# Second-layer attention product with tiles of the probabilities as weights and the solution moving

## Chip, cores and metric

The kernel runs on one core of a Trainium2 chip. The metric is the device time of one execution in microseconds (us); a kernel's time is the median of its runs. The core has five engines with queues of their own that work in order and wait for one another by semaphores: TensorE (PE in the profile, its weight loads PEld), VectorE (DVE), ScalarE (ACT), GpSimd (POOL) and SyncE (SP, which issues DMAs).

## What is computed

Two transformer layers on x of shape (4, 256, 256). Each layer has an attention and a feed-forward part, each fed by a gated recurrence over time (`cond`). In the second layer the attention doesn't multiply the probabilities with the values but with the solution u of a triangular system for each of the 16 heads (head width 16), and the feed-forward part routes each token to two of eight experts. The part that the change touches, in the reference:

```python
p = e / where(denom == 0, 1, denom)              # keys against earlier keys, row sums 1
A = p * beta + eye(T)                            # lower triangular, 256 x 256 for each head
u = solve_triangular(A, v, lower=True)
attn = softmax(where(causal, q k^T * scale, -inf))
o = einsum('bhij,bhjd->bihd', attn, u).reshape(B, T, 256)
return o @ Wo
```

## The kernel before

The four batches are worked one after the other. A list of steps, ORDER, gives the order on every engine; each engine walks through it and does its part of each step. DVE uses a variant (DVE_ORDER, made by `lag`) in which steps that don't belong to the chain of a solve are held back behind the chain's steps while a solve is under way.

The solve of a batch goes by blocks of 32 rows: `inverse` (DVE transposes the inverted diagonal blocks that POOL has worked out, L1845), `solve` (PE multiplies a block, DVE copies the result to `ublk`, L1867, SP moves it with four DMAs, L866, to `uaug`/`uflat`, where tokens lie on partitions) and `update` (PE, L1138; DVE, L1853 and L1856) in turn, eight blocks in two halves. Other work of the batches around it (scores and probabilities, projections, `oT` and `wo` of the batch before) is spread between the chain's steps by `spread`.

Behind each chain stands `pv`, the product of probabilities and solution, on PE in two steps of eight heads (L1054 to L1070). The probabilities `prob` lie with keys on partitions, in full floats and not yet divided by their sums. For each head the weights are 32 columns of `uflat` (16 of the solution, one of ones that yields the sum, 15 that belong to the next head), and the moving operand is `prob[:, h, 0:256]` for the first 128 keys and the last 128 queries for the other keys. The outputs of four heads lie in four groups of 32 partitions of a PSUM bank, so a head's values come out on partitions and the queries along the row. Both steps wait for all 32 DMAs of the solution (`u_moved`).

Then ACT copies each half to SBUF (L1421, `oraw`), PE transposes it back in eight 128x128 pieces (`otr`, L1081), and DVE takes the reciprocal of the sums from PSUM (L1734) and multiplies (L1735) into `otok`, which has queries on partitions. `oT` (L1091) transposes `otok` for the output projection `wo`. For batches 0 to 2 the `otr` steps lie among the steps of the next batch's chain; for the last one they follow at once. The next batch's `inverse` and `solve` follow `pv` in ORDER; for batches 0 and 1 some of the `kprobs` steps stand around it, and ahead of the last `pv` stand three `route` steps (tokens as 128x128 float weights, 8 columns of the gate moving) and `count`.

PSUM banks are handed out by rings: a step takes the next slot of its ring and waits until the engine named in RINGS has given it back. `mm` (L904) issues every product, so in the profile most products have one line.

Of the kernel before, what the change touches and what calls it, by code (L numbers as in the profile page):

```python
# [33 lines left out]
ALU = mybir.AluOpType  # L34
# [57 lines left out]
    ("kscores", None): ("mid", ("act",)), ("kdiag", None): ("mid", ("act",)), ("kprobs", None): ("mid", ("act",)),  # L92
    ("pv", 0): ("big", ("act",)), ("pv", 1): ("mid", ("act",)),
    ("otr", 0): ("big", ("dve",)), ("otr", 1): ("mid", ("dve",)),
    ("oT", 0): ("big", ("act",)), ("oT", 1): ("mid", ("act",)),
# [159 lines left out]
def make_order():  # L255
# [12 lines left out]

    def otr(b):
        return [[("otr", 1, b, 0)], [("otr", 1, b, 1)]]  # L270

    def keys_then_queries(b):
# [19 lines left out]
    def inverted(b):  # L292
# [4 lines left out]
             + queries(1),  # L297
             k3 + otr(0) + d3 + p1[:4] + [[("oT", 1, 0)]] + p1[4:8] + out(0)[1:] + p1[8:] + [[("qload", 3)]] + queries(2),
             otr(1) + p2[:4] + [[("oT", 1, 1)]] + p2[4:8] + out(1)[1:] + p2[8:]
             + queries(3),  # L300
             otr(2) + p3[:4] + [[("oT", 1, 2)]] + p3[4:8] + out(2)[1:] + p3[8:]]
    for b in range(B):

# [11 lines left out]
    last = sum(out(B - 1), [])  # L315
    o += [("wfirst", 0, 0), ("otr", 1, B - 1, 0), ("otr", 1, B - 1, 1), ("wsplit", 0, 0), last[0], ("wfirst", 0, 1)] + last[1:]
    o += [("wfirst", 1, 0), ("wsplit", 0, 1), ("route", B - 1)] + [("ytok", i) for i in range(B)] + [("xtok", i) for i in range(B)]
# [113 lines left out]
def program(nc, d):  # L431

    with ExitStack() as ctx:
# [104 lines left out]

        def oraw(layer, b):


            return v3(oraw0 if layer == 0 else invT[b % 2], 4)


        top_all = top[0]
# [29 lines left out]
        tern_flat = take(CT * HID, at=r1 + 4 * (H * T // 2))  # L575
        oraw0 = take(QT * H * 32, at=r1 + 5 * (H * T // 2))
        hid = v3(tern_flat, MT)
# [146 lines left out]
        pad_ready = sem("zero_columns_ready")  # L724
        u_moved = sem("solution_moved")

# [42 lines left out]
        def _(sp):  # L769
# [38 lines left out]
            for step in ORDER:  # L808
# [86 lines left out]
        def _(pe):  # L895
# [14 lines left out]
            for step in ORDER:  # L910
# [143 lines left out]
                elif kind == "pv":  # L1054
# [3 lines left out]
                    if layer == 0:  # L1058
                        wait_done(pe, ("proj", 0, b), "dve")
                        val = vflat[b % NV]  # L1060
                    else:
                        pe.wait_ge(u_moved, 16 * HQ * NS * (b + 1))
                        val = uflat
                    slot = acquire(step)
                    for h in range(step[3] * H // 2, (step[3] + 1) * H // 2) if layer else range(H):
                        out = (bank_of(slot) if layer else wide(slot)[:, h // 8, :]).rearrange("p (g t) -> p g t", g=2)[
                            (h % 4) * 32:(h % 4) * 32 + 32, h // 4 % 2, :]
                        mm(out, val[:, h * VW:h * VW + 32], prob[:, h, 0:T], True, False)
                        at = (H + h) * VW
                        last = mm(out[:, P:T], val[:, at:at + 32], prob[:, h, T:T + P], False, True)  # L1070
                    wrote(step, last)
                elif kind == "otr":

                    layer, b = step[1:3]
                    wait_done(pe, ("pv", layer, b, 1) if layer else ("pv", 0, b), "act")
                    slot = acquire(step)
                    raw = oraw(layer, b)
                    for t in step[3:] if layer else range(QT):
                        out = bank_of(slot) if layer else wide(slot)[:, t, :]
                        for g in range(4):  # L1080
                            last = nc.tensor.transpose(out[:, g * P:(g + 1) * P], raw[:, g, t * P:(t + 1) * P],  # L1081
                                                       ident)
                    wrote(step, last)
                elif kind == "oT":
                    _, layer, b = step
                    wait_done(pe, ("otr", 1, b, 1) if layer else ("otr", 0, b), "dve")
                    slot = acquire(step)
# [175 lines left out]
        def _(act):  # L1263
# [23 lines left out]
            for step in ORDER:  # L1287
# [109 lines left out]
                elif kind == "kscores":  # L1397
# [11 lines left out]
                    give_back(step, ins)  # L1409
                elif kind == "pv":  # L1410
                    layer, b = step[1:3]
                    slot = filled(step)
                    if layer == 0:
                        if b:
                            wait_pe(act, ("otr", 0, b - 1))
                    else:
                        wait_pe(act, ("solve", b, NS - 1, 1))
                        act.wait_ge(invT_ready, b + 1)
                    if layer:
                        half = slice(2 * step[3], 2 * step[3] + 2)  # L1420
                        give_back(step, A(oraw(layer, b)[:, half, :], bank_of(slot).rearrange("p (g t) -> p g t", g=2), ACT.Copy))  # L1421
                    else:
                        give_back(step, A(oraw(layer, b), wide(slot).rearrange("p a (g t) -> p (a g) t", g=2), ACT.Copy))
                elif kind == "oT":
# [94 lines left out]
        def _(dve):  # L1519
# [50 lines left out]
            for step in DVE_ORDER:  # L1570
# [139 lines left out]
                elif kind == "minus":  # L1710
# [11 lines left out]
                    V.tensor_tensor(lo, v3(mneg, QT), hi, ALU.subtract).then_inc(mparts_ready["max"], 1)  # L1722
                elif kind == "otr":
                    layer, b = step[1:3]
                    slot = filled(step)
                    n = layer * B + b
                    ts = slice(step[3], step[3] + 1) if layer else slice(0, QT)
                    nt = ts.stop - ts.start
                    o_ = (v3(bank_of(slot), 1) if layer else wide(slot)).rearrange("p t (h e) -> p t h e", h=H)
                    if n:  # L1730
# [4 lines left out]
                    give_back(step, V.tensor_tensor(otok[:, ts].rearrange("p t (h e) -> p t h e", h=H), o_[:, :, :, 0:HD],  # L1735
                                                    r_.unsqueeze(3).to_broadcast([P, nt, H, HD]), ALU.mult))
                elif kind == "wo":
# [101 lines left out]
                elif kind == "inverse":  # L1839
# [340 lines left out]
```

## Time and profile before

| | us |
|---|---|
| median of 3 runs | 781.09 (777.92 to 781.1) |
| the profiled execution | 783.57 |
| its span, first to last instruction | 781.8 |
| PE busy with products | 512.3 |
| PE busy with weight loads | 416.5 |
| DVE busy | 566.9 |
| ACT busy | 329.5 |
| POOL busy | 214.1 |

The second layer's solves and attention lie between about 425 and 640 us of the span. Times in rows count from the start of the span. Each float product on PE shows as two rows, a pass each, with a weight load of its own. "128*32" is the part of the array that a product uses (rows times columns), "128x256" the moving operand. PEclk is the granted clock of TensorE as a share of 2.4 GHz; it has two levels, 1.0 and 0.5. "idle before" in brackets is how long the engine stood still and what ended that.

### The profile page before, as it was taken

How to read it: one execution, taken by the hardware profiler on the slowest of the kernel's cores; microseconds unless marked ns; L12 is line 12 of the kernel's file. 1: busy time of each engine (PE TensorE's matmuls, PEld its weight loads, DVE VectorE, ACT ScalarE, POOL GpSimd, SP SyncE). 2: the span in 40 equal slices, each digit the busy share in tenths (PEclk: the TensorE clock that was granted, in tenths of full speed). 3: DMA queues.
4: the chain of work that ended last, by engine and by line, in shares of the span. 5: the costliest groups of instructions: out<-in, count | busy, mean ns of one | idle time of the engine just before them, and what ended most of it. 6: DMA issues, size and time to landing. Idle time of an engine off the chain costs nothing.

```text
span 781.8 us, 17527 instructions
## 1 busy us (share of the span) xinstructions
PE 512.3 (66%) x7117; PEld 416.5 (53%) x7117; DVE 566.9 (73%) x1184; ACT 329.5 (42%) x779; POOL 214.1 (27%) x313
## 2 busy tenths in 40 slices
PE   0451754895595853444647577758887873799995
PEld 0341643784485742332435355536654653799995
DVE  6899599797859994678676877666475446768861
ACT  4335243453355622006365611433411343368771
POOL 3000000000000000000685881880683001325443
PEclk9965656896798977665667676659898856699999
DMA  8055005032000020175007133002202238256622
GB/s 310 22 118 122 0 18 105 1 85 38 1 2 1 1 55 0 49 156 122 4 3 158 13 75 61 7 5 49 64 10 63 31 143 283 88 153 204 191 29 27
DMA packets 48209, 56.02 MB, mean 72 GB/s; under 512 B 25136, under 2 KB 42048, under 8 KB 43648
## 3 DMA queue, kind: packets, MB, share of 16 engines
q1 hardware_dynamic: 44784, 49.90, 24.7%
q0 software_dynamic: 3344, 4.99, 3.4%
q8 instruction: 56, 0.92, 0.5%
q14 instruction: 25, 0.20, 0.1%
HBM read 43.15 MB, written 10.49 MB: 69 GB/s over the span
## 4 chain that ended last, share of the span: by engine, by line
PE 37%; DVE 27%; issue 8%; ACT 4%; DMA 1%; POOL 1%; SPq 0%; POOLq 0%; DVEq 0%; ACTq 0%
PE psum L904 32%; DVE arena L1705 3%; PE psum L1138 3%; DVE arena L1687 2%; DVE arena L1856 2%; ACT psum L1408 1%; DVE arena L1692 1%; DVE arena L1695 1%; DVE arena L1693 1%; DVE arena L1853 1%; DVE arena L1590 1%; DVE arena L1618 1%; DVE arena L1634 1%; DVE psum L1654 1%; DVE arena L1655 1%
## 5 line engine op out<-in xcount | busy, mean ns | idle before, releaser
L904 PE MATMUL psum<-arena 32*32 32x16 f32 (+20 forms) x5281 | 354.6, 278 | 192.1 <-DVE arena L1634 76.6
L904 PEld LDWEIGHTS psum<-arena 98*32 98x32 bf16 (+8 forms) x5281 | 273.6, 128 | 269.7 <-DVE arena L1634 79.3
L2086 POOL TENSOR_TENSOR arena<-arena 128x31 f32<-128x31 f32 (+15 forms) x124 | 69.0, 556 | 9.7
L1705 DVE TENSOR_REDUCE arena<-psum 128x4 f32<-128x1024 f32 (+2 forms) x80 | 59.7, 789 | 11.6 <-PE psum L904 11.1
L1373 ACT ACTIVATE arena<-psum 128x512 f32<-128x512 f32 (+1 forms) x80 | 50.5, 687 | 40.0 <-PE psum L904 40.0
L2084 POOL TENSOR_TENSOR arena<-arena 128x31 f32<-128x31 f32 (+15 forms) x124 | 64.4, 520 | 9.7
L1408 ACT ACTIVATE psum<-psum,arena 128x256 f32<-128x256 f32 (+7 forms) x128 | 45.3, 367 | 27.8 <-DVE arena L1695 27.5
L1604 DVE TENSOR_TENSOR_SCAN arena<-arena 128x255 f32<-128x255 f32 x64 | 42.5, 727 | 11.4 <-ACT arena L1318 11.3
L2065 POOL DMA_DIRECT2D arena<-wq x1 | 0.9, 862 | 171.9 <-PE psum L904 171.9
L1318 ACT ACTIVATE arena<-arena 128x255 f32<-128x255 f32 x64 | 27.2, 498 | 46.4 <-DVE arena L1590 46.4
L2110 POOL DMA_INDIRECT out<-arena x16 | 31.2, 1948 | 48.9 <-DVE arena L2010 46.8
L2100 POOL DMA_INDIRECT arena<-dispatched,arena x16 | 19.6, 1227 | 84.7 <-DVE arena L1977 81.0
L1992 DVE TENSOR_TENSOR fc_second_parts<-arena,fc_first_parts 128x2048 fp32r<-128x2048 f32 x16 | 36.6, 2290 | 7.8 <-ACT fc_first_parts L1515 7.7
L904 PE MATMUL psum<-input_first_parts,fc_first_parts 128*128 128x256 f32 x128 | 39.0, 305 | 1.3 <-DVE input_second_parts L1986 1.3
L1487 ACT ACTIVATE psum<-psum,arena 128x256 f32<-128x256 f32 x64 | 24.6, 448 | 35.7 <-PE psum L904 35.7
L1138 PE MATMUL psum<-arena 32*32 32x224 f32 (+6 forms) x896 | 36.2, 307 | 5.0 <-DVE arena L1867 3.0
L1590 DVE TENSOR_TENSOR_SCAN arena<-arena 128x256 f32<-128x256 f32 x64 | 39.0, 672 | 0.5
L904 PE MATMUL psum<-fc_first_parts,hidden_first_parts 128*128 128x256 f32 x128 | 36.8, 288 | 2.5 <-DVE hidden_second_parts L2003 2.5
L904 PE MATMUL psum<-input_second_parts,fc_first_parts 128*128 128x256 f32 x128 | 38.2, 299 | 0.0
L904 PE MATMUL psum<-input_first_parts,fc_second_parts 128*128 128x256 f32 x128 | 38.2, 298 | 0.0
L904 PE MATMUL psum<-fc_first_parts,hidden_second_parts 128*128 128x256 f32 x128 | 36.2, 283 | 0.0
L904 PE MATMUL psum<-fc_second_parts,hidden_first_parts 128*128 128x256 f32 x128 | 36.2, 283 | 0.0
(185 smaller groups left out, 890.4 us busy)
## 6 DMA issues: line engine op xcount, KB each, us to landing
arena<-fc SPq DMA_DIRECT2D x16, 1024.0 KB, 5.0
arena<-parts SPq DMA_DIRECT2D x40, 256.0 KB, 4.6
parts<-arena SPq DMA_DIRECT2D x16, 384.0 KB, 3.6
arena<-parts SPq DMA_DIRECT2D x40, 128.0 KB, 5.5
arena<-arena SPq DMA_DIRECT2D x128, 8.0 KB
arena<-xT SPq DMA_DIRECT2D x1, 1024.0 KB, 10.4
arena<-w1T SPq DMA_DIRECT2D x1, 1024.0 KB, 10.8
arena<-w2T SPq DMA_DIRECT2D x1, 1024.0 KB, 13.0
```

What stands on the lines that cost most here:

```text
L904: return nc.tensor.matmul(out, lhsT, rhs, start=start, stop=stop)
L1138: last = nc.tensor.matmul(acc(half)[rows, qq, (s + 1) * BLK:T], ublk[rows, s, q, :], later[b % 2][s][rows, q, :], start=s == 0 and qq == 0 ...
L1318: A(scan[s + 1][:, ct, 0:T - 1], scan[s][:, ct, 0:T - 1], ACT.Copy, scale=back[:, i:i + 1]).then_inc(scaled, 1)
L1373: ins = A(prob[:, first:end, 0:T] if early else prob[:, first:end, T:T + P], src, ACT.Exp, scale=scale)
L1408: ins = A(s_, s_, ACT.Exp, bias=nbias[:, n:n + 1], accum_out=ncc[b][:, n:n + 1])
L1590: ins = V.tensor_tensor_scan(scan[s][:, ct, :], dd, src[:, ct, bt(b)], 0.0, ALU.mult, ALU.add)
L1604: st(V.tensor_tensor_scan(scan[s][:, ct, T - 2::-1], dd, scan[s + 1][:, ct, T - 2::-1], scan[s][:, ct, T - 1:T], ALU.mult, ALU.add))
L1705: ins = V.tensor_reduce(mneg[:, at + first:at + end], src, axis=AX.X, op=ALU.max, negate=True)
L1992: V.tensor_tensor(second[:], fcw[e % NW][i], first[:].bitcast(F32), ALU.subtract).then_inc(w_second[i], 1)
L2084: link(G_.tensor_tensor(tmp, A3[:, k + 1:BLK, k:k + 1].to_broadcast([P, rows, w]), X3[:, k:k + 1, 0:w].to_broadcast([P, rows, w]), ALU.mult))
L2086: ins = G_.tensor_tensor(X3[:, k + 1:BLK, 0:w], X3[:, k + 1:BLK, 0:w], tmp, ALU.add)
L2110: G_.indirect_dma_start(out=d["out"], out_offset=bass.IndirectOffsetOnAxis(ap=ids[:, 2 * e + s:2 * e + s + 1], axis=0), in_=eo[e % 2][:, s ...
```

## The change

In the second layer `pv` is done with the operands in each other's place: the weights are a 128x128 tile of `prob` (128 keys by 128 queries of one head), the moving operand is the 17 columns of a head in `uflat` (16 of the solution and the one of ones). The two steps of `pv` are now the two halves of the queries, each for all 16 heads, with queries on partitions: the first has one tile of keys, the second two, which add up in PSUM. DVE reads the result where `pv` has left it and takes the reciprocal and the product as before. The `otr` steps of the second layer go, and with them ACT's copies; `pv` is given back by DVE and so stands in DVE's order, right behind the chain and ahead of the next `inverse`. The semaphore `u_moved` becomes one for each tile of 128 keys. `inverse` of a later batch waits for the last `solve` instead of `otr`, and at the end ACT's first conversion of expert weights waits for the last `pv`. The first layer stays as it is. The diff, cut to its core:

```diff
-    ("pv", 0): ("big", ("act",)), ("pv", 1): ("mid", ("act",)),
-    ("otr", 0): ("big", ("dve",)), ("otr", 1): ("mid", ("dve",)),
+    ("pv", 0): ("big", ("act",)), ("pv", 1): ("mid", ("dve",)),
+    ("otr", 0): ("big", ("dve",)),
...
-             k3 + otr(0) + d3 + p1[:4] + [[("oT", 1, 0)]] + p1[4:8] + out(0)[1:] + p1[8:] + [[("qload", 3)]] + queries(2),
-             otr(1) + p2[:4] + [[("oT", 1, 1)]] + p2[4:8] + out(1)[1:] + p2[8:]
+             k3 + d3 + p1[:4] + [[("oT", 1, 0)]] + p1[4:8] + out(0)[1:] + p1[8:] + [[("qload", 3)]] + queries(2),
+             p2[:4] + [[("oT", 1, 1)]] + p2[4:8] + out(1)[1:] + p2[8:]
              + queries(3),
-             otr(2) + p3[:4] + [[("oT", 1, 2)]] + p3[4:8] + out(2)[1:] + p3[8:]]
+             p3[:4] + [[("oT", 1, 2)]] + p3[4:8] + out(2)[1:] + p3[8:]]
...
-    o += [("wfirst", 0, 0), ("otr", 1, B - 1, 0), ("otr", 1, B - 1, 1), ("wsplit", 0, 0), last[0], ("wfirst", 0, 1)] + last[1:]
+    o += [("wfirst", 0, 0), last[0], ("wsplit", 0, 0), ("wfirst", 0, 1)] + last[1:]
...
-        u_moved = sem("solution_moved")
+        u_moved = [sem(f"solution_tile{t}_moved") for t in range(QT)]
...
-                                     ).then_inc(u_moved, 16)
+                                     ).then_inc(u_moved[t], 16)
...
                     else:
-                        pe.wait_ge(u_moved, 16 * HQ * NS * (b + 1))
-                        val = uflat
-                    slot = acquire(step)
-                    for h in range(step[3] * H // 2, (step[3] + 1) * H // 2) if layer else range(H):
-                        out = (bank_of(slot) if layer else wide(slot)[:, h // 8, :]).rearrange("p (g t) -> p g t", g=2)[
-                            (h % 4) * 32:(h % 4) * 32 + 32, h // 4 % 2, :]
-                        mm(out, val[:, h * VW:h * VW + 32], prob[:, h, 0:T], True, False)
-                        at = (H + h) * VW
-                        last = mm(out[:, P:T], val[:, at:at + 32], prob[:, h, T:T + P], False, True)
+                        t = step[3]
+                        slot = acquire(step)
+                        for kt in range(t + 1):
+                            pe.wait_ge(u_moved[kt], 16 * HQ * NB * (b + 1))
+                            for h in range(H):
+                                at = (kt * H + h) * VW
+                                queries = slice(T, T + P) if kt else slice(t * P, (t + 1) * P)
+                                last = mm(bank_of(slot)[:, h * VW:(h + 1) * VW], prob[:, h, queries], uflat[:, at:at + VW],
+                                          kt == 0 and h == 0, kt == t and h == H - 1)
...
-                        wait_pe(act, ("solve", b, NS - 1, 1))
-                        act.wait_ge(invT_ready, b + 1)
-                    if layer:
-                        half = slice(2 * step[3], 2 * step[3] + 2)
-                        give_back(step, A(oraw(layer, b)[:, half, :], bank_of(slot).rearrange("p (g t) -> p g t", g=2), ACT.Copy))
...
                 elif kind == "wfirst" or kind == "wsplit" and step[1] >= 2:
                     _, e, i = step
+                    if e == 0:
+                        wait_pe(act, ("pv", 1, B - 1, 1))
...
-                elif kind == "otr":
+                elif kind == "otr" or kind == "pv" and step[1]:
...
-                    o_ = (v3(bank_of(slot), 1) if layer else wide(slot)).rearrange("p t (h e) -> p t h e", h=H)
+                    if layer:
+                        o_ = v3(bank_of(slot)[:, 0:H * VW], 1).rearrange("p t (h e) -> p t h e", h=H)
...
                     if b >= 2:
-                        wait_pe(dve, ("otr", 1, b - 2, 1))
+                        wait_pe(dve, ("solve", b - 2, NS - 1, 1))
...
                     if b and s == 0:
-                        dve.wait_ge(u_moved, 16 * HQ * NS * b)
+                        for t in range(QT):
+                            dve.wait_ge(u_moved[t], 16 * HQ * NB * b)
```

## Rows read from the trace of the kernel before

**Rows 1.** The page: its first line, and the chain that ended last, by engine.

```profile
span 781.8 us, 17527 instructions
...
PE 512.3 (66%) x7117; PEld 416.5 (53%) x7117; DVE 566.9 (73%) x1184; ACT 329.5 (42%) x779; POOL 214.1 (27%) x313
...
PE 37%; DVE 27%; issue 8%; ACT 4%; DMA 1%; POOL 1%; SPq 0%; POOLq 0%; DVEq 0%; ACTq 0%
```

**Rows 2.** Timeline after batch 0: start, us, engine, line, op, tiles, xcount [idle before].

```profile
488.57 6.60 PE L904 MATMUL psum<-arena 128*32 128x256 f32 x152 [1.01 <-issue]
...
493.89 0.60 ACT L1421 ACTIVATE arena<-psum 128x512 f32<-128x512 f32 x1 [1.83 <-PE psum L904]
...
494.55 0.30 DVE L1867 COPY arena<-psum 128x32 f32<-128x32 f32 x2 [7.83 <-PE psum L904]
```

**Rows 3.** Timeline, handover after batch 1.

```profile
549.45 1.97 DVE L1845 STREAM_TRANSPOSE arena<-arena 128x1024 f32<-128x1024 f32 x1
...
551.57 1.91 POOL L2077 TENSOR_TENSOR arena<-arena 128x1024 f32<-128x1024 f32 x1 [22.08 <-DVE arena L1845]
...
552.48 0.24 PEld L904 LDWEIGHTS psum<-arena 128*32 128x32 f32 x4 [0.18 <-issue]
...
557.42 0.29 DVE L1867 COPY arena<-psum 128x32 f32<-128x32 f32 x2 [6.00 <-PE psum L904]
```

**Rows 4.** Timeline, handover after batch 2.

```profile
589.71 0.31 PE L1033 MATMUL psum<-arena 128*64 128x128 bf16 x1 [2.50 <-DVE arena L1722]
...
593.35 1.97 DVE L1845 STREAM_TRANSPOSE arena<-arena 128x1024 f32<-128x1024 f32 x1 [3.69 <-POOL arena L2086]
...
596.88 0.30 DVE L1867 COPY arena<-psum 128x32 f32<-128x32 f32 x2 [1.56 <-PE psum L904]
```

**Rows 5.** Timeline, last batch: routing, product, normalising, transposition of the result.

```profile
619.08 11.48 PE L904 MATMUL psum<-arena 32*32 32x16 f32 x113 [0.26 <-DVE arena L1856]
...
632.08 0.26 DVE L1734 RECIPROCAL arena<-psum 128x16 f32<-128x16 f32 x1 [6.05 <-PE psum L1081]
...
632.37 0.42 DVE L1735 TENSOR_TENSOR arena<-psum,arena 128x256 f32<-128x256 f32 x1
...
633.47 0.72 PEld L1091 LDWEIGHTS psum<-arena 128*128 128x128 f32 x4 [1.29 <-DVE arena L1735]
```

**Rows 6.** Groups by form, 625.5 to 630.6: shapes, xcount, busy us, mean ns.

```profile
L904 PEld LDWEIGHTS psum<-arena 128*32 128x32 f32 x64 | 3.0, 159 | 1.8 <-issue 1.5
```

**Rows 7.** Stretches: us, busy PE, PEld, DVE, ACT, POOL, PEclk, DMA, GB/s.

```profile
488.60:493.80 5.20, 5.20 (x81) 3.68 (x85) 0.00 (x0) 0.72 (x2) 4.44 (x10) 0.53 0.00 0
...
501.00:524.00 23.00, 10.79 (x301) 7.22 (x302) 16.23 (x50) 11.90 (x60) 20.41 (x34) 0.50 0.05 5
...
597.00:619.00 22.00, 19.05 (x488) 12.73 (x488) 12.86 (x63) 7.19 (x13) 0.00 (x0) 1.00 0.12 13
...
620.40:625.20 4.80, 4.80 (x25) 4.79 (x24) 0.70 (x4) 0.67 (x2) 0.00 (x0) 0.50 0.39 72
...
625.60:630.60 5.00, 4.96 (x65) 3.03 (x64) 0.35 (x2) 0.88 (x2) 0.00 (x0) 0.56 1.02 431
```

**Rows 8.** Groups by form, 620.3 to 625.2, the routing products.

```profile
L904 PEld LDWEIGHTS psum<-arena 128*128 128x128 f32 x24 | 5.4, 333 | 0.1
...
L904 PE MATMUL psum<-arena 128*128 128x8 f32 x24 | 5.1, 355 | 0.0
```

**Rows 9.** Timeline, a transposition of the second layer at full clock.

```profile
597.26 0.42 PEld L1081 LDWEIGHTS psum<-arena 128*128 128x128 f32 x4 [0.48 <-ACT arena L1421]
```

**Rows 10.** Timeline of PE alone: products of the chains of batches 1 and 3.

```profile
524.05 2.36 PE L1138 MATMUL psum<-arena 32*32 32x160 f32 x32 [1.78 <-issue]
...
597.85 1.72 PE L1138 MATMUL psum<-arena 32*32 32x224 f32 x32
...
615.90 0.45 PE L1138 MATMUL psum<-arena 32*32 32x32 f32 x32
```

**Rows 11.** Timeline, products of ranks with bf16 weights.

```profile
648.42 1.21 PEld L904 LDWEIGHTS psum<-arena 128*128 128x128 bf16 x40
```

More of the change, by code:

```diff
@@ L267, in pv @@
         return [("pv", 1, b, 0), ("pv", 1, b, 1)]
-    def otr(b):
-        return [[("otr", 1, b, 0)], [("otr", 1, b, 1)]]
     def keys_then_queries(b):
@@ L537, in program @@
         top[0] = max(top[0], e_end)
-        def oraw(layer, b):
-            return v3(oraw0 if layer == 0 else invT[b % 2], 4)
         top_all = top[0]
@@ L575, in program @@
         tern_flat = take(CT * HID, at=r1 + 4 * (H * T // 2))
-        oraw0 = take(QT * H * 32, at=r1 + 5 * (H * T // 2))
+        oraw0 = v3(take(QT * H * 32, at=r1 + 5 * (H * T // 2)), 4)
         hid = v3(tern_flat, MT)
@@ new lines, in _ @@
+                        for h in range(H):
+                            out = wide(slot)[:, h // 8, :].rearrange("p (g t) -> p g t", g=2)[(h % 4) * 32:(h % 4) * 32 + 32, h // 4 % 2, :]
+                            mm(out, val[:, h * VW:h * VW + 32], prob[:, h, 0:T], True, False)
+                            at = (H + h) * VW
+                            last = mm(out[:, P:T], val[:, at:at + 32], prob[:, h, T:T + P], False, True)
+                    else:
+                        t = step[3]
+                        slot = acquire(step)
+                        for kt in range(t + 1):
+                            pe.wait_ge(u_moved[kt], 16 * HQ * NB * (b + 1))
+                            for h in range(H):
+                                at = (kt * H + h) * VW
+                                queries = slice(T, T + P) if kt else slice(t * P, (t + 1) * P)
+                                last = mm(bank_of(slot)[:, h * VW:(h + 1) * VW], prob[:, h, queries], uflat[:, at:at + VW],
+                                          kt == 0 and h == 0, kt == t and h == H - 1)
@@ L1071, in _ @@
                     wrote(step, last)
                 elif kind == "otr":
-                    layer, b = step[1:3]
-                    wait_done(pe, ("pv", layer, b, 1) if layer else ("pv", 0, b), "act")
+                    _, layer, b = step
+                    wait_done(pe, ("pv", layer, b), "act")
                     slot = acquire(step)
-                    raw = oraw(layer, b)
-                    for t in step[3:] if layer else range(QT):
-                        out = bank_of(slot) if layer else wide(slot)[:, t, :]
+                    raw = oraw0
@@ L1080, in _ @@
+                    for t in range(QT):
                         for g in range(4):
-                            last = nc.tensor.transpose(out[:, g * P:(g + 1) * P], raw[:, g, t * P:(t + 1) * P],
+                            last = nc.tensor.transpose(wide(slot)[:, t, g * P:(g + 1) * P], raw[:, g, t * P:(t + 1) * P],
                                                        ident)
@@ L1085, in _ @@
                     _, layer, b = step
-                    wait_done(pe, ("otr", 1, b, 1) if layer else ("otr", 0, b), "dve")
+                    wait_done(pe, ("pv", 1, b, 1) if layer else ("otr", 0, b), "dve")
                     slot = acquire(step)
@@ L1409, in _ @@
                     give_back(step, ins)
-                elif kind == "pv":
-                    layer, b = step[1:3]
+                elif kind == "pv" and step[1] == 0:
+                    b = step[2]
                     slot = filled(step)
[L1413 to L1416, printed above, removed]
-                        wait_pe(act, ("solve", b, NS - 1, 1))
-                        act.wait_ge(invT_ready, b + 1)
-                    if layer:
-                        half = slice(2 * step[3], 2 * step[3] + 2)
-                        give_back(step, A(oraw(layer, b)[:, half, :], bank_of(slot).rearrange("p (g t) -> p g t", g=2), ACT.Copy))
-                    else:
-                        give_back(step, A(oraw(layer, b), wide(slot).rearrange("p a (g t) -> p (a g) t", g=2), ACT.Copy))
+                    if b:
+                        wait_pe(act, ("otr", 0, b - 1))
+                    give_back(step, A(oraw0, wide(slot).rearrange("p a (g t) -> p (a g) t", g=2), ACT.Copy))
                 elif kind == "oT":
@@ L1727, in _ @@
                     ts = slice(step[3], step[3] + 1) if layer else slice(0, QT)
-                    nt = ts.stop - ts.start
-                    o_ = (v3(bank_of(slot), 1) if layer else wide(slot)).rearrange("p t (h e) -> p t h e", h=H)
+                    if layer:
+                        o_ = v3(bank_of(slot)[:, 0:H * VW], 1).rearrange("p t (h e) -> p t h e", h=H)
+                    else:
+                        o_ = wide(slot).rearrange("p t (h e) -> p t h e", h=H)
                     if n:
@@ L1735, in _ @@
                     give_back(step, V.tensor_tensor(otok[:, ts].rearrange("p t (h e) -> p t h e", h=H), o_[:, :, :, 0:HD],
-                                                    r_.unsqueeze(3).to_broadcast([P, nt, H, HD]), ALU.mult))
+                                                    r_.unsqueeze(3).to_broadcast([P, ts.stop - ts.start, H, HD]), ALU.mult))
                 elif kind == "wo":
@@ L1865, in _ @@
                     if b and s == 0:
-                        dve.wait_ge(u_moved, 16 * HQ * NS * b)
+                        for t in range(QT):
+                            dve.wait_ge(u_moved[t], 16 * HQ * NB * b)
                     give_back(step, V.tensor_copy(ublk[:, s, half * QP:(half + 1) * QP, 0:HD],
```

## The prediction

> **What bounds the kernel now.** I read the page first: the span, the busy shares and the chain that ended last. No engine is full (TensorE, PE in the rows, is busy 66% of the 781.8 us), but the chain lies on PE for 37% and on VectorE (DVE) for 27% [rows 1]: work is handed to and fro, and time counts where the chain passes. So I went by the timeline to the four places where the change acts, the second layer's attention product `pv` of each of the four batches. In the first three, one solve chain has just ended and the next one starts with `inverse` (a transposition on DVE) and `solve`, whose first result is copied by L1867; on PE's queue, which runs in the order of ORDER, the next `solve` stands behind `pv`. The reader is to see in [rows 2 to 4] that PE has nothing beside `pv` there: batch 0's product starts at 488.57, after 1.01 us of waiting for the last rows of the solution, its second eviction starts at 493.89, and the next chain's first copy comes at 494.55. In the last batch [rows 5] PE runs without a gap from 619.08 to 630.56 (three `route` steps, then `pv`), then an eviction, eight transpositions, and normalising on DVE before `oT` starts at 633.47. So `pv` is on the path in all four places, and what it costs on PE is paid in full.
>
> Then I asked the list of groups by form what one `pv` is now, and the view by stretches which clock it gets. It is 64 loads of 128x32 weights [rows 6], because each of its 32 float products is done in two passes; four of them stand side by side in the array. The last batch's fills a stretch of 5.0 us, the first one's 5.2 us, both at a granted clock just over 0.5, that is 1.2 GHz for most of it [rows 7]. Its end is later followed by full clock: 597 to 619 has 1.00 [rows 7].
>
> **The change part by part.** *The product.* Per batch the new `pv` does 16 heads for the first half of the queries and 2 x 16 for the second: 48 products, each with a 128x128 tile of probabilities as weights and 17 columns moving. In two passes that is 96 loads of 128x128 float weights. The trace of before has the same load with almost as few moving columns: `route`, 128x128 float weights and 8 columns. There, 24 passes kept PE busy 5.1 us [rows 8], 0.2125 us each, with no idle time, at clock 0.50 [rows 7]. The moving columns don't show in that pace: one load lasts 333 ns on average [rows 8], longer than the distance to the next, so loads set it. I take the same price for 17 columns: 96 x 0.2125 = 20.4 us for a batch, where 5.0 to 5.2 us stood. A lower bound for a pass is the full-clock row: four 128x128 float loads of a transposition took 0.42 us [rows 9] in a stretch at clock 1.00 [rows 7], 0.105 each, 10.1 us for a batch. An upper bound is a little over the 0.2125. I take the end at half rate, because `route` is the same form, and because it shows what such a stream does to the clock: it ran 4.8 us without a gap and stayed at 0.50 [rows 7], and the old `pv` that followed was still mostly there. The stretches ahead of `pv` are sparse, as they are now, and nothing in the change makes them denser, so it starts at the low level too.
>
> The Trainium skill (TensorE: Matmul & The Clock Gate, section on what is actually happening) says that sustained matmul activity releases the throttle. By that rule the new `pv`, four times as long as the old one and without a gap, would run at 2.4 GHz for most of its length; the `route` stretch at 0.50 [rows 7] speaks against it. The same page (section LDWEIGHTS) prices a load by its columns over 1.2 GHz, an estimate of 107 ns for 128 of them; the `route` row [rows 8] has twice that. By either the sum would be that of the first rival below.
>
> *The wait for the solution.* The semaphore is split by tile, and only the last third of `pv` needs the second tile. The 1.01 us of batch 0 [rows 2] goes, and in batch 2 `pv` can start right after 590.02, where PE's last step ahead of it ends [rows 4]. Nothing is queued behind this wait that could gain more.
>
> *The handover to the next chain.* ACT's two copies and the eight transpositions go; DVE now reads PSUM, a reciprocal and a multiplication for each half, 0.26 and 0.42 us [rows 5]. The first half's lie under PE, the second's 0.7 us follow PE's end. This is a new place on DVE's queue: `inverse` of the next batch stands behind `pv`, so DVE waits for PE some 20 us with the transposition of 1.97 us [rows 3] queued behind it, and PE's first `solve` waits for that. Before, it was done while PE multiplied or waited. From the end of `pv` to the first copy of the next chain I count 0.7 + 1.97 + 0.6 (a `solve` and its handover, an estimate from the 0.66 us between the last eviction's start and the copy, 493.89 to 494.55 [rows 2]) = 3.3 us.
>
> Now the four places, new against old:
> - batch 0: 487.56 + 20.4 + 3.3 = 511.3 against 494.55 [rows 2], +16.7
> - batch 1: 552.48 + 20.4 + 3.3 = 576.2 against 557.42 [rows 3], +18.8
> - batch 2: 590.02 + 20.4 + 3.3 = 613.7 against 596.88 [rows 4], +16.8
> - batch 3: the old product's end, 630.56, less its 5.0 [rows 5, 7], is 625.6; 625.6 + 20.4 + 0.7 = 646.7 against 633.47 for `oT` [rows 5], +13.2
>
> Together +65.5 us. GpSimd's inversion of a batch starts when the one before is handed over (551.57 [rows 3]) and ends at 593.35 [rows 4], some 42 us, which made DVE wait 3.69 us in batch 2. It starts late now too, but the chain plus the longer `pv` that it has to be ready for is longer by 20 us, so it stays covered; were it not, it would cost what is left of 3.69 us.
>
> *What the chains gain.* In the chains of batches 1 to 3 the eight transpositions (twice 0.42 us at full clock [rows 9]) and DVE's two pairs (1.36 us [rows 5]) no longer stand among the steps: at most 2.2 us a chain, nothing where they filled a wait. I take 1.3 for each, -4 us, with 0 and -6.6 as ends.
>
> *What the clock does afterwards.* The old `pv` ended with the clock on its way up. After a stream like `route` the next chain starts at the low level. A step of the chain's products took 2.36 us with 160 columns in chain 1, at the low level, and 1.72 with 224 in chain 3, at the high one [rows 7, 10]: 14.8 ns a column against 7.7. Chain 3 has seven such rows, from 1.72 down to 0.45 us [rows 10], 7.5 us together, of 19.05 us that PE is busy there [rows 7]. A whole chain at half rate would lose 7.5 us on these and, as I estimate, 5 of the 11.5 on the rest, the remainder lying in waits for DVE. Chain 1 is mostly low already (501 to 524 at 0.50 [rows 7]), so two chains bear it: 0 to 25 us. I take +7, under a third, since the `proj`, `probs` and `wo` steps that lie in these chains are those in which the clock stands high now.
>
> The rest has one answer: SP's semaphores count differently but the same DMAs go out at the same steps; ACT's first conversion of expert weights waits for the end of `pv`, where it stood behind the copies of the same product; the PSUM ring has two uses fewer per batch. I cost these at nothing, because `oT`, `wo` and the gate follow in the same order and hide the conversions as now.
>
> Sum: 65.5 - 4 + 7 = +68.5 us. The profiled execution took 783.57 us around its span of 781.8; the median of the three runs is 781.09, 2.5 below it. On the profiled execution the sum gives 852, on the median 849.6; I forecast 850.
>
> **The rivals.**
> 1. *The stream itself lifts the clock.* Then a pass costs 0.105 us [rows 9], a `pv` 10.1 us instead of 20.4, and nothing is lost afterwards: 65.5 - 4 x 10.3 - 4 = +20.3, 801 us; lifted for part of each batch, 812 to 840. For it: four places of 20 us of dense PE, more than any stretch there now. Against it: `route` [rows 7]. It decides from the batch in which the clock rises within the stream. This is also the time by the two rules of the skill.
> 2. *Faster: loads at the price of bf16.* The table of ranks does 40 passes with 128x128 bf16 weights in 1.21 us [rows 11], 0.03 each. At that price a new `pv` is 2.9 us: 65.5 - 4 x 17.5 - 4 = -8.5, 773 us. It decides below about 0.05 us for a pass, where 65.5 - 4 is paid back over 384 passes. Against it: the operands stay float, and the float row with 8 columns is at 0.2125. Only if the second pass reused a loaded tile, or loads lay side by side, could it come near.
> 3. *The low clock spreads.* The chains of batches 2 and 3 stay at half rate to their ends, and the dense stretches after them too: +25 instead of +7 and more, 868 us and above.
>
> That the change doesn't do what it says is hardly a case: the rows of the copies and of `otr` can't stay, since the steps are gone from the order.
>
> **How the numbers follow.** Forecast (half rate, 850, its own range 840 to 871): 0.70. Rival 1: 0.20, of which 0.08 for full rate throughout and 0.12 for part. Rival 2: 0.04, nearly all of it faster. Rival 3: 0.06. The range from 812 to 870 leaves out the full-rate case, rival 2 and most of rival 3, 0.18 or so. A measurement of this kernel can tell about 0.5% (4 us) from no change; faster 0.03, same 0.01, slower 0.96.
>
> **What would show it.** In the profile of after: a group of 128x128 float loads with 17 columns, 384 passes in all, four stretches of about 20 us of PE with a granted clock of 0.50 (rival 1: 1.00 and 10 us); DVE idle for most of each, ended by PE, and `inverse` right behind; no gap on PE ahead of `pv` in batch 0; the four shifts near 17, 19, 17 and 13 us; low clock at the start of the chains of batches 2 and 3. I am wrong if the stream's pace with 17 columns isn't that with 8, or if PE's queue lets other work in between.

## The result and the profile after

The changed kernel takes 848.63 us (843.05 to 852.44), the kernel before 779.77 beside it: a ratio of 1.0875, 95% interval 1.0836 to 1.0914. The profiled execution took 849.38 us around a span of 847.6, with a mean granted clock of 0.751 (before: 0.774).

The page of after: span, busy times, and the group in which DVE's waiting now lies.

```profile
span 847.6 us, 17700 instructions
...
PE 571.7 (67%) x7213; PEld 480.5 (57%) x7213; DVE 568.2 (67%) x1184; ACT 324.5 (38%) x771; POOL 214.8 (25%) x313
...
L1727 DVE RECIPROCAL arena<-psum 128x16 f32<-128x16 f32 (+1 forms) x12 | 3.4, 286 | 84.5 <-PE psum L895 84.5
```

Against [rows 1] PE is busy 59.4 us longer and its weight loads 64.0 us, while DVE is nearly as before (1.3 us more) and ACT 5.0 us shorter (the copies that went). DVE's 84.5 us of waiting ahead of the reciprocals of the second layer (two for each `pv`; the other four are the first layer's) all end with a product: this is the four new `pv`, seen from their reader.

The stretches of after: the four `pv`, then the start and the rest of the chains of batches 2 and 3. Columns as in [rows 7].

```profile
488.40:509.00 20.60, 20.60 (x104) 20.56 (x104) 0.68 (x2) 1.20 (x6) 0.00 (x0) 0.50 0.00 1
567.70:588.30 20.60, 20.60 (x100) 20.56 (x104) 0.68 (x2) 1.35 (x6) 0.00 (x0) 0.50 0.16 53
624.90:645.60 20.70, 20.69 (x97) 20.55 (x96) 0.68 (x2) 0.27 (x1) 6.65 (x17) 0.50 0.16 53
677.70:698.30 20.60, 20.60 (x98) 20.49 (x97) 1.03 (x4) 0.28 (x1) 0.00 (x0) 0.50 0.36 139
591.50:596.80 5.30, 5.30 (x47) 2.50 (x43) 2.42 (x8) 1.16 (x2) 4.76 (x7) 0.50 0.07 6
596.80:622.40 25.60, 20.78 (x506) 14.15 (x505) 19.04 (x62) 6.46 (x13) 22.58 (x38) 1.00 0.10 10
648.80:651.60 2.80, 2.64 (x36) 1.35 (x32) 0.93 (x5) 0.00 (x0) 0.00 (x0) 0.52 0.08 12
651.60:672.00 20.40, 17.58 (x477) 11.63 (x470) 11.21 (x54) 7.57 (x13) 0.00 (x0) 1.00 0.12 12
```

Each `pv` fills PE for 20.6 us at the lower level, where [rows 7] has 5.0 and 5.2 (and the old `pv` of batch 1 took 3.8). The last four lines show what is left of that level behind it: the chains of batches 2 and 3 run their first 5.3 and 2.8 us at 0.50 and the rest at 1.00.

The groups by form of after: a `pv` of batch 0, and all 384 passes of the second layer.

```profile
L895 PE MATMUL psum<-arena 128*128 128x17 f32 x96 | 20.7, 375 | 0.0
L895 PEld LDWEIGHTS psum<-arena 128*128 128x128 f32 x96 | 20.6, 333 | 0.1
...
L895 PE MATMUL psum<-arena 128*128 128x17 f32 x384 | 82.6, 375 | 0.0
```

It is 82.6 / 384 = 0.215 us a pass. A load again lasts longer (333 ns) than the distance to the next, as in [rows 8].

The timeline of after: the handovers behind batches 0 and 2 and the step to `oT` in the last batch.

```profile
486.01 23.89 PE L895 MATMUL psum<-arena 98*32 98x224 bf16 x208
...
495.41 0.26 DVE L1727 RECIPROCAL arena<-psum 128x16 f32<-128x16 f32 x1 [9.71 <-PE psum L895]
...
509.07 0.26 DVE L1727 RECIPROCAL arena<-psum 128x16 f32<-128x16 f32 x1 [12.94 <-PE psum L895]
509.36 0.42 DVE L1728 TENSOR_TENSOR arena<-psum,arena 128x256 f32<-128x256 f32 x1
...
509.70 1.90 DVE L1838 STREAM_TRANSPOSE arena<-arena 128x1024 f32<-128x1024 f32 x1
511.65 1.39 PEld L895 LDWEIGHTS psum<-arena 32*32 32x32 f32 x56 [1.97 <-DVE arena L1838]
...
512.19 0.35 DVE L1861 COPY arena<-psum 128x32 f32<-128x32 f32 x2 [0.59 <-DVE arena L1838]
...
645.63 0.26 DVE L1727 RECIPROCAL arena<-psum 128x16 f32<-128x16 f32 x1 [12.94 <-PE psum L895]
...
646.26 1.89 DVE L1838 STREAM_TRANSPOSE arena<-arena 128x1024 f32<-128x1024 f32 x1
...
648.75 0.35 DVE L1861 COPY arena<-psum 128x32 f32<-128x32 f32 x2 [0.59 <-DVE arena L1838]
...
673.79 24.51 PE L895 MATMUL psum<-arena 128*128 128x8 f32 x115
...
698.34 0.26 DVE L1727 RECIPROCAL arena<-psum 128x16 f32<-128x16 f32 x1 [12.88 <-PE psum L895]
...
699.11 0.72 PEld L1087 LDWEIGHTS psum<-arena 128*128 128x128 f32 x4 [0.92 <-DVE arena L1728]
```

The first line is `kprobs` of batch 1 and `pv` of batch 0 without a gap, so the 1.01 us of [rows 2] is gone. At 509.07 PE is done, DVE normalises, and only then its transposition comes (L1838, `inverse`), with PE waiting 1.97 us for it. The first copy of the next chain stands at 512.19, where [rows 2] has 494.55. Behind batch 2 it is the same picture. In the last batch `oT` starts at 699.11.

The whole, cut at the first and last copy of each chain (L1861 in after, L1867 in before):

| | before | after | difference |
|---|---|---|---|
| start to first copy of chain 0 | 427.30 | 428.18 | +0.9 |
| chains 0, 1, 2, 3 | 55.48, 52.34, 30.11, 22.58 | 55.49, 50.59, 30.90, 23.26 | 0.0, -1.75, +0.8, +0.7 |
| handovers behind batches 0, 1, 2 | 11.77, 10.52, 9.36 | 28.52, 28.68, 26.38 | +16.75, +18.2, +17.0 |
| last copy of chain 3 to the end | 162.29 | 175.56 | +13.3 |

The four places of the change make up 65.2 of the 65.8 us between the spans.

### The profile page after: what moved, and what is told of

It reads as the page before. It is cut to its first block and busy times, and to the rows that moved or that the text cites. A ratio compares the mean times of both kernels' runs of the same rounds, so it can differ in the third digit from the quotient of the medians.

```text
span 847.6 us, 17700 instructions
## 1 busy us (share of the span) xinstructions
PE 571.7 (67%) x7213; PEld 480.5 (57%) x7213; DVE 568.2 (67%) x1184; ACT 324.5 (38%) x771; POOL 214.8 (25%) x313
## 5 line engine op out<-in xcount | busy, mean ns | idle before, releaser
L895 PE MATMUL psum<-arena 32*32 32x16 f32 (+21 forms) x5409 | 416.8, 276 | 199.6 <-DVE arena L1624 76.5
L895 PEld LDWEIGHTS psum<-arena 128*128 128x128 f32 (+8 forms) x5409 | 341.8, 142 | 271.0 <-DVE arena L1624 79.2
L1695 DVE TENSOR_REDUCE arena<-psum 128x4 f32<-128x1024 f32 (+2 forms) x80 | 59.8, 788 | 10.8 <-PE psum L895 10.4
L1727 DVE RECIPROCAL arena<-psum 128x16 f32<-128x16 f32 (+1 forms) x12 | 3.4, 286 | 84.5 <-PE psum L895 84.5
L1505 ACT ACTIVATE fc_first_parts<-arena 128x2048 fp32r<-128x2048 f32 x16 | 30.6, 1910 | 32.6 <-PE psum L895 32.6
L1134 PE MATMUL psum<-arena 32*32 32x224 f32 (+6 forms) x896 | 39.4, 323 | 4.8 <-DVE arena L1861 4.7
L2071 POOL TENSOR_TENSOR arena<-arena 128x1024 f32<-128x1024 f32 x4 | 7.6, 1909 | 126.3 <-DVE arena L1838 82.9
```

The source lines that it names most:

```text
L895: return nc.tensor.matmul(out, lhsT, rhs, start=start, stop=stop)
L1134: last = nc.tensor.matmul(acc(half)[rows, qq, (s + 1) * BLK:T], ublk[rows, s, q, :], later[b % 2][s][rows, q, :], start=s == 0 and qq == 0 ...
L1505: A(w_parts[i][e % 2][0][:], fcw[e % NW][i], ACT.Copy).then_inc(w_first, 1)
L1695: ins = V.tensor_reduce(mneg[:, at + first:at + end], src, axis=AX.X, op=ALU.max, negate=True)
```

## The experiments

The theory was the prediction's: a pass costs its weight load, 0.213 us at the lower clock level (0.50), whether 8 or 17 columns move through it, and that level stays. The rivals: moving columns or accumulation set the pace; the new order on DVE's queue is to blame; not the load but the exchange of operands as such is bad. The before beside each group of runs: 781.76 us for `a_w17`, `a_w128`, `a_inv` and `a_bf16`, 780.06 for `b_split`, `b_bf16` and `a_bf16_inv`, 780.51 for `a_w128_inv`.

**More columns through the same loads.** `a_w17` is a control, the changed kernel with `pv` head by head; `a_w128` moves up to 128 columns, of which the first 17 are wanted and the rest is overwritten by the heads that follow.

```diff
-for kt in range(t + 1):
+for kt in range(QT):
     pe.wait_ge(u_moved[kt], 16 * HQ * NB * (b + 1))
-    for h in range(H):
+for h in range(H):
+    n = min(128, QT * H * VW + 32 - VW - (t * H + h) * VW)      # a_w17: min(17, ...)
+    for kt in range(t + 1):
...
-        mm(bank_of(slot)[:, h * VW:(h + 1) * VW], prob[:, h, queries], uflat[:, at:at + VW], kt == 0 and h == 0, kt == t and h == H - 1)
+        mm(bank_of(slot)[:, h * VW:h * VW + n], prob[:, h, queries], uflat[:, at:at + n], kt == 0, kt == t)
```

> The kernel after the change, with the products head by head (both key tiles of a head one after the other) and a wait for both tiles of the solution ahead of the product. It is the control for the run with 128 columns. Theory (96 loads of 128x128 float weights at 0.213 us each set the pace, at the low clock): the order of the products doesn't matter; the product still lasts 20.4 us a batch; the earlier wait costs at most 1.0 us in batch 0 and about 1.6 in batch 2, so 849 to 852 us. Rival (it is the adding up in PSUM, 16 open heads in one bank, that sets the pace): the stretches change by more than 2 us each.

849.86 us (848.16 to 851.87), ratio 1.0864 (1.0823 to 1.0906): the control takes as long as the changed kernel. Its streams take 20.5 to 20.6 us at 0.50 too.

> As the control, but each product moves up to 128 columns instead of 17 (the head's 17 and those of the heads after it, whose results are overwritten by the next head's own; the last heads have fewer). Same 96 loads a batch, up to seven times the columns. Theory (loads set the pace; moving columns run beside the next load): at the low clock 128 columns take about 0.21 us a pass, by half of the 0.427 us of a 256-column pass, so the product stays near 20.4 us a batch and the time near 850; if the denser stream gets the high clock, a pass is about 0.107 us, the product 10 to 13 us a batch, and the time 805 to 825 us: faster with more work. Rival (columns and loads follow one another): 111 more columns at two passes, 96 x 0.185 us = 17.8 us more a batch, about 920 us.

820.06 us (815.72 to 820.9), ratio 1.0465 (1.042 to 1.051): with up to seven times the columns it is 30 us faster. The stretches of its first `pv`:

```profile
488.40:493.00 4.60, 4.60 (x22) 4.60 (x23) 0.00 (x0) 0.00 (x0) 0.00 (x0) 0.50 0.00 0
493.00:501.40 8.40, 8.40 (x80) 8.36 (x83) 0.68 (x2) 0.00 (x0) 0.00 (x0) 1.00 0.01 2
```

And the groups by form of the second stretch:

```profile
L895 PEld LDWEIGHTS psum<-arena 128*128 128x128 f32 x73 | 8.2, 192 | 0.0
```

For 4.6 us the stream ran at 0.50, 22 passes of 0.21 us each, the pace of 17 columns and of 8; then at 1.00, 73 loads in 8.2 us, 0.112 each. The four streams took 13.1, 12.9, 13.15 and 13.5 us. So columns don't set the pace at either level; in both stretches the loads are busy without a break (4.60 of 4.60 us, 8.36 of 8.40), and they do. (No run makes such a float pass without its load, so "load" stands for all that a pass pays apart from its columns.) The price that the first rival put on the full level, 0.105, was near, and 820 lies in its range for a clock that rises within the stream (812 to 840). What failed it is its condition: with 17 columns the level never rose. Which property of the wider stream matters is left open; the runs vary the columns alone.

**`inverse` ahead of `pv` on DVE's queue.**

```diff
 DVE_ORDER = lag(...)
+for _b in range(B - 1):
+    DVE_ORDER.remove(("inverse", _b + 1))
+    DVE_ORDER.insert(DVE_ORDER.index(("pv", 1, _b, 0)), ("inverse", _b + 1))
```

> The kernel after the change, with the next batch's inverse transposed ahead of the product's two steps in the order of DVE (one part of the change undone: the place of the transposition). Theory (each handover is 20.4 us of product plus 0.7 of normalising plus 1.97 of the transposition, all on the path): the last two go off the path in three handovers, 2.0 to 2.7 us each, 841 to 843 us. Rival (something else is late too, the last probabilities or GpSimd's inversion): 847 to 849 us.

838.02 us (836.33 to 840.89), ratio 1.0717 (1.0673 to 1.0761), a shorter time than expected. Timeline of DVE behind batch 0:

```profile
484.37 1.99 DVE L1841 STREAM_TRANSPOSE arena<-arena 128x1024 f32<-128x1024 f32 x1
...
507.83 0.26 DVE L1730 RECIPROCAL arena<-psum 128x16 f32<-128x16 f32 x1 [12.88 <-PE psum L898]
...
508.12 0.42 DVE L1731 TENSOR_TENSOR arena<-psum,arena 128x256 f32<-128x256 f32 x1
...
509.06 0.41 DVE L1864 COPY arena<-psum 128x32 f32<-128x32 f32 x2 [0.52 <-PE psum L898]
```

The transposition now lies ahead of the stream, and the copy comes 0.52 us after normalising. The handovers became 1.9, 1.4 and 2.7 us shorter, 6.0 together, near the 2.0 to 2.7 each of the theory. The kernel gained 10.6 us (its span 11.2); the rest lies in stretches that the edit doesn't touch (up to the first copy -1.4, chain 1 -0.8, chain 2 -2.9, chain 3 +2.3, tail -2.5) and isn't explained by it; chains 2 and 3 had a granted clock of 0.95 and 0.82 here and of 0.91 and 0.94 in after. The order on DVE's queue is worth about 2 us a batch, of the 17 to 18 that a handover grew.

**Both together.**

> The changed kernel with up to 128 columns moving (820.1 us) and the next inverse transposed ahead of the product on DVE (838.0 us alone). It is the best form of the new operand order that keeps full floats. Theory (load price and handover are separate terms that add, and the loads alone, 96 of 0.107 us at the high clock, keep it above the kernel before): 809 to 814 us. Rival (at the high clock the loads hide and only the handover was left): below 795 us.

802.82 us (800.15 to 805.0), ratio 1.0272 (1.0223 to 1.0322), 17.2 below `a_w128`, more than expected. The handovers give 2.5, 3.0 and 3.4 us of it, and the chains of batches 2 and 3 another 3.3 and 3.4. Stretches of these two chains:

```profile
570.80:597.90 27.10, 23.40 (x549) 15.77 (x548) 19.73 (x70) 8.01 (x17) 23.92 (x41) 1.00 0.10 11
615.00:637.10 22.10, 19.23 (x501) 12.70 (x502) 12.14 (x60) 7.57 (x13) 0.00 (x0) 0.97 0.12 13
```

The same chains in `a_w128`:

```profile
576.60:607.00 30.40, 26.30 (x552) 16.91 (x548) 21.25 (x70) 7.62 (x14) 26.97 (x44) 0.89 0.09 10
627.40:653.00 25.60, 22.73 (x511) 13.78 (x504) 12.22 (x60) 7.57 (x13) 0.00 (x0) 0.83 0.10 11
```

They had 0.89 and 0.83, behind a pause of PE of 2.1 and 2.6 us while DVE normalised and transposed; in `a_w128_inv` PE goes from the stream to the chain with no pause over 0.6 us, and the level that the stream had reached lasted through nearly all of the chain. That the pause is the reason is argued from one profiled execution of each. This is the fastest form of the new product in full floats that ran, and it is still 22 us above the kernel before: 96 passes at 0.112 us are 10.8 us a batch, twice the 5.0 to 5.2 of [rows 7].

**The load at another price.** The changed kernel, with the upper halves of both operands read as bf16, where they lie; and the same in the kernel before.

```diff
+probs_high = prob_flat.bitcast(BF16).rearrange("p (h t two) -> p h t two", h=H, two=2)
+u_high = uflat.bitcast(BF16).rearrange("p (n two) -> p n two", two=2)
-    mm(..., prob[:, h, queries], uflat[:, at:at + VW], ...)
+    mm(..., probs_high[:, h, queries, 1], u_high[:, at:at + VW, 1], ...)
```

> The kernel after the change, but both operands of the product are read as bf16, the upper halves of the floats: 48 passes a batch with bf16 loads instead of 96 with float ones; everything else, order and handover too, is as after. The product is less exact. Theory (the price is that of the float loads): 48 passes at 0.06 to 0.107 us, 2.9 to 5.1 us a batch, so 849 - 4 x (15.3 to 17.5) = 779 to 788 us. Rival (the loss comes from the handover and the new waits, not from the loads): above 810 us.

777.65 us (775.17 to 781.16), ratio 0.9957 (0.993 to 0.9984), a little under what was expected. Groups by form of the second layer:

```profile
L895 PE MATMUL psum<-arena 128*128 128x17 bf16 x192 | 6.2, 177 | 2.4 <-DMA arena<-arena 2.4
```

192 passes (one for each product) in 6.2 us, 0.032 each, where the float passes took 0.215. The stretch of the first `pv` shows that this is at the lower level:

```profile
488.20:490.10 1.90, 1.63 (x60) 1.50 (x56) 0.68 (x2) 1.25 (x6) 0.00 (x0) 0.50 0.01 0
```

A `pv` takes 1.6 us, and the loss of some 70 us is gone, though the order of the steps is that of the changed kernel. The timeline behind batch 2 shows what is late next:

```profile
590.09 0.59 PE L895 MATMUL psum<-arena 128*128 128x17 bf16 x16 [2.10 <-DMA arena<-arena]
...
595.50 1.91 DVE L1840 STREAM_TRANSPOSE arena<-arena 128x1024 f32<-128x1024 f32 x1 [4.06 <-POOL arena L2082]
```

First PE waits 2.10 us for the second tile of the solution, then DVE 4.06 us for GpSimd's inversion, which the long stream had covered.

> The kernel before, with both operands of the second layer's product read as bf16 (upper halves of the floats), in the old positions: 32 passes a batch in four column groups instead of 64, copies and transpositions as before. The product is less exact. With the run of the changed kernel on bf16 (777.7 us) it takes the price of float loads out of the comparison of the two operand orders. Theory (what the change saves beside the loads is one eviction, a transposition and a handover in the last batch and little in the others, since the chain waits for GpSimd or DVE there): the old product falls from 5.0 to about 1.3 us, 3 to 4 us in batches 0, 1 and 3 and nothing in batch 2, so 769 to 773 us: the old order is not worse even without the load price. Rival (the new order pays once loads are cheap): above 779 us.

775.06 us (772.1 to 777.97), ratio 0.9938 (0.9908 to 0.9967), a gain of 5.0 where 7 to 11 were expected. In its profile the handovers changed by -3.1, -2.3 and +0.8 us and the tail by -3.7, near the 3 to 4 that were expected of batches 0, 1 and 3; chains 2 and 3 were 0.5 and 1.2 longer. The same change of price is worth 5 us with the operands in their old places and 71 (848.63 to 777.65) in the new ones.

> The changed kernel on bf16, with the next inverse transposed ahead of the product on DVE. Theory (in the changed kernel the transposition of 1.97 us and 0.7 us of normalising are on the path in each handover, and GpSimd's inversion of batch 3, which made DVE wait 4.06 us in the run on bf16, starts earlier with it): 2.0 to 2.7 us in batches 0 and 1 and 2 to 5 in batch 2, 768 to 772 us. Rival (the handover is bound elsewhere once the product is short, by the solution's DMA wait of 2.1 us): 775 to 778 us.

`a_bf16` with `inverse` ahead of `pv`: 772.72 us (771.33 to 773.74), ratio 0.9894 (0.9851 to 0.9938), a little above what was expected. Handovers 2.3, 1.9 and 1.4 us shorter, the last below the 2 to 5 expected: behind batch 2 DVE waits longer for the inversion:

```profile
586.51 1.91 DVE L1843 STREAM_TRANSPOSE arena<-arena 128x1024 f32<-128x1024 f32 x1 [6.48 <-POOL arena L2085]
```

So with cheap loads the new product stands 2.6 us above the old one as it is (777.65 against 775.06) and 2.3 below it with the transposition moved. The comparison isn't of the operands alone: the new one has the split wait (next run), the old one hasn't. The exchange of operands loses above all by what float products pay for their loads; the place on DVE's queue adds about 2 us a batch.

**The split wait alone.** The kernel before, in full floats, with `u_moved` for each tile of keys as in the change, and `pv` of eight heads working through the first tile before it waits for the second:

```diff
-pe.wait_ge(u_moved, 16 * HQ * NS * (b + 1))
...
+for kt in range(QT):
+    pe.wait_ge(u_moved[kt], 16 * HQ * NB * (b + 1))
+    for n, h in enumerate(mine):
...
+        mm(out[:, kt * P:T], val[:, at:at + 32], prob[:, h, kt * T:T + kt * P], kt == 0 and n < 4, kt == 1 and n >= 4)
```

> One part of the change alone, on the kernel before: the solution's semaphore is split by tile, and each step of the old product does its eight heads' first key tile before it waits for the second. Operands, copies and transpositions stay as before. Theory (in the change this part is worth the waits that end the solve, 1.0 us in batch 0 and up to 1.6 in batch 2, and GpSimd's inversion still ends late in batch 2): 778 to 781 us against about 781. Rival (the split is what makes the new order good, and the loads eat a larger gain): 775 us or less.

773.63 us (771.68 to 783.32), ratio 0.9911 (0.9877 to 0.9946), below both kernels in full floats, by more than expected, and in the range of the rival (775 or less). The handovers are 2.3, 0.2 and 1.1 us shorter, and the tail 4.4. Stretches of the first two `pv`:

```profile
486.90:490.90 4.00, 4.00 (x96) 2.65 (x88) 0.00 (x0) 1.77 (x6) 3.63 (x5) 0.70 0.00 0
547.90:551.90 4.00, 4.00 (x84) 2.54 (x80) 0.00 (x0) 1.55 (x5) 3.63 (x5) 0.65 0.58 236
```

The first takes 4.0 us at 0.70 where [rows 7] has 5.2 at 0.53. The second is no faster than in the kernel before:

```profile
552.50:556.30 3.80, 3.80 (x81) 2.88 (x77) 0.00 (x0) 1.53 (x5) 3.44 (x4) 0.68 0.63 250
```

The timeline of the last batch in `b_split`, `wo` and the last `route`:

```profile
629.63 1.99 PE L904 MATMUL psum<-arena 128*128 128x256 f32 x8 [0.69 <-ACT arena L1439]
...
633.85 1.06 PE L904 MATMUL psum<-arena 128*128 128x8 f32 x8 [2.23 <-DVE arena L1643]
```

The same eight passes of each in the timeline of before:

```profile
635.28 3.78 PE L904 MATMUL psum<-arena 128*128 128x256 f32 x8 [0.69 <-ACT arena L1430]
...
641.29 1.88 PE L904 MATMUL psum<-arena 128*128 128x8 f32 x8 [2.23 <-DVE arena L1634]
```

They take nearly twice the time: the clock stood high in the tail of `b_split` and low in that of before. So the removed wait gives the 2 us or so that were expected, and most of the rest goes with the clock. It isn't one profiled execution that caught it high: the nine runs had a mean granted clock of 0.777 to 0.793, median 0.787, and the twenty of the kernel before beside them 0.772 to 0.788, median 0.7785. Why it is higher isn't shown. Nor is the rival excluded, that the split is what the new order has in its favour: of the kernels on bf16 only the changed ones have it, and no run takes it out of the changed kernel.

## Why the prediction was right

**The product** was the term that mattered: 0.2125 us a pass from `route` against 0.215 measured, 20.4 us a batch against 20.6. `a_w128` bears out the reason given: the pace at 17 columns is that at up to 128, and PE's loads fill it. Taking the bound at half rate rather than the full-clock one [rows 9] was the choice that decided, and the ground for it, that `route` had not lifted the clock [rows 7], held for a stream four times as long: in after, `a_w17` and `a_inv` all twelve streams of 17 columns stayed at 0.50 to their ends. Rows 7 alone could not show that. In `a_w128` the level rose after 4.6 us, about as long as `route` had run, so 4.8 us at 0.50 didn't exclude a rise later; a chance of 0.20 stood for it.

The Trainium skill (TensorE: Matmul & The Clock Gate, section on what is actually happening) says that activity releases the throttle. The four streams of 20.6 us at 0.50 don't follow that rule, and `a_w128`, at 1.00 after 4.6 us, does. The same page of the Trainium skill (section LDWEIGHTS) prices a load by its columns over 1.2 GHz, an estimate of 107 ns for 128 of them; passes with a float load had 0.112 us at the upper level and 0.215 at the lower one, so for them the figure fits the upper level alone. Its section on weight-path perf modes says that a fast weight load is on for 128 weights of any type but FP32, and gives it about a factor of two. The runs agree on which type gains, 0.032 against 0.215 us a pass at the same level. That factor, 6.7, is between two types; no run has a bf16 load without the fast one, so none shows the page's factor.

**The waits and the handover.** The 1.01 us went. From the end of `pv` to the next copy I counted 3.3 us; 509.00 to 512.19 is 3.2. `inverse` behind `pv` on DVE's queue costs 2 us a batch, as `a_inv` showed by moving it. Shifts forecast 16.7, 18.8, 16.8 and 13.2, measured 16.75, 18.2, 17.0 and 13.3: 65.5 against 65.2. GpSimd's inversion stayed covered, since the transposition of batch 3 (646.26) follows normalising at once; `a_bf16` showed what it costs without that cover, 4.06 us.

**Chains and clock.** Forecast -4 and +7, together +3; chains 1 to 3 gave -0.3. The low level stood at the start of chains 2 and 3, as forecast, but the 7 was too much: half speed over 5.3 and 2.8 us can cost at most half of that, 2.65 and 1.4, about 4 us. What the missing steps give shows best in chain 1, with the clock at 0.74 before and after: 1.75 us, where I took 1.3. In chains 2 and 3 the two terms aren't separated. With the `otr` steps gone and the clock at 1.00 and 0.97 they took 27.15 and 22.16 us in `a_w128_inv`, 3.75 and 1.1 less than in after, and the 3.75 is more than the low stretch can cost. In `a_w17`, with the streams of after, chain 2 took 29.71 and not 30.90, so one profiled execution of each doesn't settle a microsecond here.

**The sum.** +68.5 was forecast against the profiled execution, 852.1; 849.4 was measured. Of the 2.7 us the terms of the chains are 3.3 and the four places 0.3, less 0.9 that came ahead of the first chain, where nothing was forecast. On the medians the kernel lost 68.9 us (848.63 against 779.77), which is nearer to the sum than the 65.8 between the profiled spans. So it is in part luck that 850 came within 1.4 us: the profiled execution of before, 783.57, lay above all four runs beside the result (777.92 to 781.1), so the medians are 3 us further apart than the profiles, about what the terms of the chains had too much.

**The rivals.** The first had nearly the right price and the wrong condition. The second's mechanism, a load at the price of bf16, exists (`a_bf16`), but with bf16 operands; float loads never came near. Its 773 compares with 777.65; the run shows two waits behind a short `pv`, 2.10 and 4.06 us, and doesn't settle how much of the difference they are. In the third the low level would have lasted to the ends of the chains; it lasted 5.3 and 2.8 us.

## What to carry to other kernels

Before weights and moving operand change places, count the weight loads and look at how wide they are: a float product with few moving columns costs its loads, and wide tiles can't stand side by side as narrow ones do. Price the new stream by the row of the same weight form and type nearest to it, at the clock level that this row had, and ask of each level separately whether the stream will get it. Where an engine's step becomes the reader of a long product, look at what stands behind it on that engine's queue, and put what is already due ahead of it.

## What the runs showed of the hardware beside this

- The granted clock stayed at 0.50 through 20.6 us of products without a gap at 17 columns, and rose to 1.00 after 4.6 us of the same loads with up to 128 columns (`a_w128`); 30 us of the kernel's time hang on that.
- At the lower level a 128x128 load took 0.215 us in floats and 0.032 us in bf16. As a float product makes two passes, a product with 17 columns is 13 times as dear in floats.
- Behind the stream at full level, the chains of batches 2 and 3 had 0.89 and 0.83 with a pause of PE of 2.1 and 2.6 us ahead of them, and 1.00 and 0.97 without it (one profiled execution of each); they were 3.3 and 3.4 us shorter, beside the pause itself.
